# Second stage of a two-layer kernel: where the transform of the down weights stands in a tile's four steps

## What is computed

```python
x = layernorm(x + attention(x) @ Wo.T)      # linear attention, 16 heads of 128
x = layernorm(x + ffn(x))
# ffn:
x = fwht(x * SU_ug) / SCALE
u, g = x @ W_up.T * s_up, x @ W_gate.T * s_gate
h = silu(g) * u                              # width 2048
y = (fwht(h * SU_dp) / SCALE) @ W_down.T * (Wscale_dp * SCALE)
```

## Time and profile before

| | us |
|---|---|
| median of 3 runs | 2412.4 (2411.36 to 2416.23) |
| profiled execution | 2415.87 |
| its span in the trace | 2414.0 |
| TensorE matmul busy | 2266.5 (94%) |
| VectorE busy | 1846.6 (76%) |
| ScalarE busy | 1277.1 (53%) |
| GpSimd busy | 1124.7 (47%) |
| products of the second stage | 961.97 to about 1364 |
| mean granted TensorE clock | 0.978 |

### The profile page before, as it was taken

The page is one execution under the profiler, slowest core; times in us unless marked ns, Lnnn a source line. Parts: engine busy times, 40 slices in busy tenths (PEclk is TensorE's granted clock), DMA queues, the critical chain, the costliest instruction groups (busy, mean ns, idle before and its releaser), DMA issues. The chain is left out here.

```text
span 2414.0 us, 32843 instructions
## 1 busy us (share of the span) xinstructions
PE 2266.5 (94%) x10209; PEld 1826.2 (76%) x10209; DVE 1846.6 (76%) x2450; ACT 1277.1 (53%) x2281; POOL 1124.7 (47%) x999
## 2 busy tenths in 40 slices
PE   6999999999999994999999759999999999999997
PEld 5777878787777782777777548778877887788885
DVE  6877786868777774688888567887888788878876
ACT  5667666767666663233443345455444554454442
POOL 4667676767667772455445332421343034303310
PEclk9999999999999997999999889999999999999999
DMA  4011120102011105776777252223222323222312
GB/s 145 36 67 42 58 70 31 65 35 70 35 61 40 65 36 199 254 254 231 253 249 272 74 180 66 66 70 114 84 95 85 109 83 101 83 83 79 105 57 88
DMA packets 132589, 252.81 MB, mean 105 GB/s; under 512 B 44305, under 2 KB 45201, under 8 KB 122769
## 3 DMA queue, kind: packets, MB, share of 16 engines
q1 hardware_dynamic: 132496, 251.66, 30.8%
HBM read 188.18 MB, written 63.44 MB: 104 GB/s over the span
## 5 line engine op out<-in xcount | busy, mean ns | idle before, releaser
L1110 PE MATMUL pc<-xch,wch 128*128 128x512 f32 x896 | 352.0, 393 | 42.3 <-ACT u L1213 15.1
L1110 PE MATMUL pc<-xcl,wch 128*128 128x512 f32 x896 | 349.7, 390 | 0.0
L1110 PE MATMUL pc<-xch,wcl 128*128 128x512 f32 x896 | 349.6, 390 | 0.0
L1391 POOL TENSOR_TENSOR wcs<-wcr 128x256 f32<-128x256 f32 x64 | 67.9, 1061 | 582.0 <-DVE wcl L1260 554.8
L472 POOL TENSOR_TENSOR tb<-tb,sinb 128x512 f32<-128x512 f32 x160 | 221.3, 1383 | 97.0 <-ACT tb L338 96.2
L1110 PEld LDWEIGHTS pc<-xch,wch 128*128 128x128 f32 x896 | 168.8, 188 | 85.7 <-ACT u L1213 22.0
L678 PE MATMUL py<-woh,oh 128*128 128x512 f32 x512 | 203.5, 397 | 30.4 <-DVE ol L823 30.4
L255 PE MATMUL pj<-xh,wqh 128*128 128x512 f32 x512 | 203.9, 398 | 4.7 <-DVE Kf L416 2.2
L1123 PE MATMUL pc<-wdh,hh 128*128 128x512 f32 x512 | 200.3, 391 | 4.8 <-DVE hl L1370 2.9
L475 POOL TENSOR_TENSOR Ql<-tb,Qh 128x512 fp32r<-128x512 f32 x128 | 171.1, 1339 | 70.5 <-ACT Qh L347 70.5
L678 PE MATMUL py<-woh,ol 128*128 128x512 f32 x512 | 201.0, 393 | 0.0
(11 more groups left out here) (176 smaller groups left out, 5899.2 us busy)
## 6 DMA issues: line engine op xcount, KB each, us to landing
num_scratch<-no SPq DMA_DIRECT2D x128, 256.0 KB, 2.4
nt<-num_scratch SPq DMA_DIRECT2D x32, 1024.0 KB, 5.3
rb<-rden_scratch SPq DMA_DIRECT2D x32, 1024.0 KB, 6.8
wdr<-wd_scratch SPq DMA_DIRECT2D x128, 256.0 KB, 3.4
wcr<-in_wg SPq DMA_DIRECT2D x64, 256.0 KB, 2.8
wcr<-in_wu SPq DMA_DIRECT2D x64, 256.0 KB, 3.1
xst<-in_xT SPq DMA_DIRECT2D x34, 256.0 KB, 3.7
xr<-in_x SPq DMA_DIRECT2D x32, 256.0 KB, 5.6
```

The costliest lines, as they stand in the source:

```text
L1110: last = nc.tensor.matmul(bank[:, :], a[n % 2][:, w, c, :], b[:, i, c, :], start=(start and k == 0), stop=(k == 5), skip_group_check=True)
L1391: nc.gpsimd.tensor_tensor(sum_w(1), raw_w(n, "u0"), raw_w(n, "u1"), ALU.add).then_inc(w_sum, 1)
```

## The change

GpSimd's rounds go one to each step. The upper and lower part of the weights are made in step 0 of the next tile (for the last tile, behind the steps). SP's load of the next columns goes to step 3, behind the two stores. The product, its eviction and its store keep their steps.

```diff
 # ScalarE, step
                 if j == 3 and at >= NCH:
                     evict(m - 1)
-                if j == 3:
-                    fold_hi(m)
+                if j == 0 and at >= NCH:
+                    fold_hi(m - 1)
...
             steps(act, step)
+            fold_hi(NM - 1)
             columns(1, NCH - 1, NC - 1, None)
 # VectorE
+            def fold_lo(q):
+                dve.wait_ge(f_hi, q + 1)
+                nc.vector.tensor_tensor(flat(fl[:]), flat(fb[:]), f32(flat(fh[:])), ALU.subtract).then_inc(f_lo, 1)
...
                 if at + 2 < NC:
                     divide(s, n + 2, m * 2 + j // 2 + 1)
-                if j == 3:
-                    dve.wait_ge(f_hi, m + 1)
-                    nc.vector.tensor_tensor(flat(fl[:]), flat(fb[:]), f32(flat(fh[:])), ALU.subtract).then_inc(f_lo, 1)
+                if j == 0 and at >= NCH:
+                    fold_lo(m - 1)
                 if j in (1, 2) and at >= NCH:
                     butterflies(m - 1, j - 1)
...
             norm(1, NC - 1)
+            fold_lo(NM - 1)
             butterflies(NM - 1, 0)
 # GpSimd, step
                 if j == 0:
                     scaled(m)
-                if j < 2:
-                    sums(m, 2 * j)
-                    sums(m, 2 * j + 1)
+                sums(m, j)
 # SP, step
-                if j == 2:
+                if j == 3 and at >= NCH:
+                    store_down(m - 1)
+                    sp.wait_ge(had_free, m * DC)
+                    sp.dma_start(x2_d[m - 1], x2[:, :, :]).then_inc(x2_out, 16)
+                if j == 3:
                     sp.wait_ge(f_step, m * 10 + 10)
                     if at + NCH < NC:
                         cols = slice((m + 1) * QC, (m + 2) * QC) if isinstance(m, int) else bass.ds(m * QC + QC, QC)
                         sp.dma_start(fa[:, :, :], wd[:, :, cols]).then_inc(f_in, 16)
-                if j == 3 and at >= NCH:
-                    store_down(m - 1)
-                    sp.wait_ge(had_free, m * DC)
-                    sp.dma_start(x2_d[m - 1], x2[:, :, :]).then_inc(x2_out, 16)
```

## The result

The changed kernel takes 2421.43 us (median of 9 runs, 2419.55 to 2426.22) against 2412.4 us (9 runs, 2410.41 to 2416.23): ratio 1.0039, with a 95% interval of 1.0028 to 1.0049. It is 9 us slower; 12.5 were forecast. The profiled execution took 2424.37 us, its span is 8.5 us longer than the one before (2422.5 against 2414.0).

What follows compares the result with a forecast made beforehand. TensorE bounds the second stage, held by the chain to its transposes. Tiles 1 to 6 at +2.0 us give 12.2, plus 0.5, plus 1.2, less 1.4: 12.5 us on the 2412.4 median, 2425 us; range 2411 to 2438.

Steps and rivals of the forecast that it cites:

- The bound and the loop: Second stage: TensorE bounds; the scaling waits for the previous tile's lower part, made 1.4 us into step 1, delaying the root.
- The rival that the root overtakes the additions: GpSimd in step 1: root ends before 7.3 us, steady tiles' waits go, about -7 us, 2405.5 us; chance 0.12.
- Step 1: Steady tile's second step: transposes wait 2.0 us where 0.43 stood, root ending at 9.25 us; +1.6 us a tile.
- Step 2: Steady tile's third step: normalised rows ready at 8.1 us, under the 9.0 needed, so no wait; -0.36 us a tile.
- the faster rival: Root through early in step 1: 7 x 0.79 = 5.5 us won in tiles, 1.4 at the end; chance 0.12.
- Step 3: Steady tile's last step: VectorE's L823 collides with the last round's second addition, transposes at 9.8 instead of 9.0; +0.8 us.
- the extra of tile 1: Tile 1 loses about 0.5 us more than other steady tiles, having no wait of 0.43 us to start from.
- The end: After the last tile's steps: lower part no longer stands in front of the last residual sum; -1.4 us.
- the last wait: TensorE's final wait for normalised rows, 5.43 us before: 1.4 us shorter, the residual sum starting near 1365.2 instead of 1366.7.
- Tile 7: Last tile: has no L823 in step 3, so it was put at +1.2 us.
- the rival of the late load: SP's load of fa starts only once the store ahead has landed: 0.9 us late a tile, 2431 us; chance 0.06.
- The clock: Rival: TensorE's clock falls in the new 2 us gap of each of seven tiles, adding 11 us, 2436 us; chance 0.10.

Runs made afterwards that it cites:

- e2: Changed kernel with the additions back in steps 0 and 1, two rounds each, and the load of fa in step 2: 2447.13 us, ratio 1.0147.
- e3: Changed kernel with ScalarE making the upper part of the weights ahead of its copies of the transposes in step 0, not behind: 2401.01 us, ratio 0.9954.
- e4: Changed kernel with an own buffer for the fourth round's result, so the scaling doesn't wait for the lower part; positions unchanged: 2402.63 us, ratio 0.9962.
- e1: Kernel before with one round of additions per step and the load of fa in step 3, upper and lower part left in step 3: 2403.86 us, ratio 0.9968.
- e5: Changed kernel with ScalarE's split of the tokens moved behind the upper part of the next chunk in step 3: 2415.87 us, ratio 1.0018.

## Why the prediction was right

**The bound and the loop.** That the scaling would sit behind the lower part until 1.4 us into step 1 is what the trace shows (1.5). e2, e3 and e4 show that this wait is the cause: made longer, made short, and cut. The rival that the root overtakes the additions asked for a root before 7.3 us into step 1; it ends at 9.1 (forecast 9.25).

**Step 1.** Forecast 2.0 us of wait, measured 1.87, +1.44 a tile instead of +1.6. **Step 2.** Forecast none, measured none; it gives back 0.52 us a tile, not 0.36, since a wait costs more than its row shows (e1). For the same reason the sentence that steady tiles have 0.79 us for any change to win is too low, and so is the price of the faster rival: e1 and e3 won 1.24 us a tile. **Step 3.** Forecast 0.8, measured 0.92 (+0.88 a tile); e5 shows the collision by itself, and e3 that it takes VectorE's lateness to bring it about. A tile was to be 2.0 us longer and is 1.8.

**The sum.** Tiles 1 to 6 with the extra of tile 1: 12.7 forecast, 12.3 measured. That agreement holds two things that offset each other: without the slow stretch in the fourth of these tiles (below) it would have been 11.7. **The end** was mis-sized: -1.3 us from the last tile and the end together, where the sum had +1.2 - 1.4 = -0.2. The term that was mis-sized is the last wait, put at 1.4 us shorter and in fact 2.2: the prediction let the residual sum begin 0.8 us behind the end of the products, and it begins at once (1376.11, the products end at 1376.08). Tile 7 itself was put at +1.2 and is +0.9. Beside the sum are 0.5 us behind the last transposes, 0.9 in tile 0, and some outside the stage. So 12.5 became 8.5 in the spans, and 9 in the medians.

**The load of fa** was no matter for the change. After it, fa lands 6.6 us after its issue in the six tiles in which a store of 1 MB is issued about 2 us before it, and 5.9 us after it in tile 0, where there is no such store; all seven waits of the scaling are for the lower part. The store itself takes 6.1 to 6.4 us. Had fa started only when the store had landed, as the rival of the late load has it, it would have landed some 3.6 us later than it did (an estimate: 1169.94 + 6.4 + 5.9 = 1182.2, against 1172.03 + 6.6 = 1178.6), and even so ahead of the scaling, which starts at 1182.7. The Trainium skill (DMA: Bandwidth & Descriptors, Rules for kernel authors) says that two such transfers serialize; in the sense in which the prediction priced this, the start of one after the landing of the other, the trace doesn't agree, and whether their data went one behind the other no run shows. Where the scaling is free to start sooner (e1, e4) the load does become what it waits for, at no cost or a small one.

**The clock.** The rival was a fall in every tile. It fell in one of seven. The stretch from the transposes of step 1 to those of step 2, in two tiles (the figure behind POOL is the granted clock):

```profile
1139.98:1152.30 12.32, 12.32 (x56) 10.22 (x57) 11.65 (x10) 2.94 (x5) 5.96 (x4) 1.00 0.45 154
1191.81:1205.75 13.94, 13.94 (x56) 11.35 (x57) 13.27 (x10) 2.94 (x5) 6.33 (x4) 0.88 0.50 183
```

Both follow a wait of 1.85 to 1.87 us. The slow one costs 1.6 us, as priced, and gives 0.9 back: that tile has no wait in step 3. That VectorE had time to catch up in the slow stretch is the likely reason.

## What to carry to other kernels

When work is moved to a later step, look at who waits for its end with an in-order queue: here GpSimd, which takes its work in order, had a wait for the previous tile's last part in front of a small operation (the root) on which the bound engine hangs, and a harmless dependence came to set the time of the tile. The place within the step decides: one call ahead of, not behind, a wait for TensorE turned +9 us into -11 us. And a wait further on in the tile may be the follow-up of the first, through lateness and a collision, so undo the first before treating the second. A wait between pipelined products costs more than the idle time in its row: compare the starts.

## What the runs showed of the hardware

Behind the waits of 1.77 to 1.89 us ahead of the transposes of step 1, TensorE's clock stayed at 2.4 GHz thirteen times and fell once: six of seven tiles of the changed kernel (0.88 over the stretch in the other) and seven of seven in e5, whose products there are just as dense. It fell once more behind 1.96 us, in tile 0 of e5 (0.50 from 984 to 986 us). Behind 4.3 to 4.4 us (e2) it fell each of seven times, and the stretch was 1.3 to 2.8 us longer each time. In the changed kernel the stretch with the fall was 1.6 us longer, and 0.9 of it came back in step 3.

The same VectorE operation (`lower`, 128 x 2048) took 2.29, 2.62 and 3.24 us as GpSimd's addition in front of it had nothing, 0.5 us or all but 0.2 us of its 1.3 us left to run. The other way round an addition took 3.22 us beside it instead of 1.29. So one of the two is held until the other is through, and they don't run side by side at a lower speed.
